# Single-precision mixing of probabilities and values in the second attention of a gated cross-attention kernel

## What is computed

```python
xn = layer_norm(x, g_x, b_x)                  # x: the context, [32, 77, 128]
ln = layer_norm(latents, g_l, b_l)            # latents: the normalised rows, [32, 128, 128]
q = jnp.einsum('bnd,de->bne', ln, Wq)
kv = jnp.einsum('bnd,de->bne', jnp.concatenate([xn, ln], axis=1), Wkv)
k, v = jnp.split(kv, 2, axis=-1)              # then split into 16 heads of 64
sim = jnp.einsum('bhid,bhjd->bhij', q * scale, k)     # 128 queries, 77 + 128 keys
attn = jax.nn.softmax(sim, axis=-1)
out = jnp.einsum('bhij,bhjd->bhid', attn, v)          # the mixing
out = out.transpose(0, 2, 1, 3).reshape(b, m, INNER) @ Wout
return layer_norm(out, g_o, b_o)
```

## Time and profile before

| | us |
|---|---|
| three executions | 1363.77, 1361.43, 1364.35 (median 1363.77) |
| profiled execution | 1359.99 |
| its span (first to last instruction) | 1358.2 |
| PE busy | 1036.5 (76%) |
| POOL busy | 889.6 (65%) |
| DVE busy | 874.3 (64%) |
| ACT busy | 859.2 (63%) |
| `attention1`: first `scores_by_key` to the last one | 478.4 to 1083.6 |
| routing tail up to the first expert tile | 1083.6 to about 1162 |
| experts | about 1162 to the end |

### The profile page before, as it was taken

How to read it: one execution, slowest core, us unless ns; L and a number is a source line. 1 busy time by engine, 2 the same in 40 slices (tenths; PEclk the granted TensorE clock), 3 DMA queues, 4 the chain that set the end, 5 groups by cost and what they waited for, 6 DMA issues and landing times. The chain is left out here.

```text
span 1358.2 us, 36485 instructions
## 1 busy us (share of the span) xinstructions
PE 1036.5 (76%) x13317; PEld 814.9 (60%) x13317; DVE 874.3 (64%) x2471; ACT 859.2 (63%) x1791; POOL 889.6 (65%) x1065
## 2 busy tenths in 40 slices
PE   1568999967894499999999999899999920566660
PEld 1445777753552278887777778777777820355550
DVE  5788788876877766666666656566665611344445
ACT  0568899964663478888877778787777810233330
POOL 1160899964767456677788888888888976144441
PEclk9869555558996599999999999999999965888985
DMA  9993000000221001112112121211212111322215
GB/s 219 261 283 85 10 16 17 16 16 12 44 43 28 1 17 34 32 28 43 33 37 50 31 59 33 53 33 38 52 34 53 33 48 48 56 58 60 63 45 187
DMA packets 210051, 78.40 MB, mean 58 GB/s; under 512 B 149663, under 2 KB 206154, under 8 KB 209883
## 3 DMA queue, kind: packets, MB, share of 16 engines
q1 hardware_dynamic: 179467, 61.91, 21.1%
q10 hardware_dynamic: 25872, 5.56, 2.3%
q0 software_dynamic: 4544, 8.67, 2.0%
HBM read 14.15 MB, written 30.47 MB: 33 GB/s over the span
## 5 line engine op out<-in xcount | busy, mean ns | idle before, releaser
L1671 DVE TENSOR_REDUCE attention_negmax<-bank 128x2 f16<-128x410 f32 x256 | 137.7, 579 | 166.3 <-PE bank L1423 164.4
L1223 POOL TENSOR_TENSOR attention_pl_l<-attention_probs_l,attention_ph_l 128x512 f16<-128x512 f32 x128 | 148.3, 1159 | 97.3 <-ACT attention_ph_l L1552 95.6
L636 POOL TENSOR_TENSOR attention_probs_l<-attention_probs,attention_probs_h 77x512 f16<-77x512 f32 x128 | 145.3, 1152 | 52.8 <-ACT attention_probs_h L718 48.5
L1223 POOL TENSOR_TENSOR attention_pl_c<-attention_probs_c,attention_ph_c 77x512 f16<-77x512 f32 x128 | 147.8, 1154 | 0.0
L1984 POOL DMA_INDIRECT outputs<-experts_y_rows,experts_ids x78 | 77.5, 994 | 102.4 <-ACT experts_y_rows L1921 87.3
L1406 PE MATMUL bank<-layer_kv,ah 128*128 128x128 f16 x1024 | 108.7, 220 | 11.7 <-PEq L2062 11.5
L1438 PEld LDWEIGHTS bank<-identh,attention_negmax 128*128 128x128 f16 (+1 forms) x1024 | 83.3, 107 | 55.9 <-issue 0.3
L1452 PE MATMUL bank<-attention_vh_l,attention_ph_l 128*128 128x65 f16 x512 | 96.0, 195 | 18.2 <-POOL attention_pl_c L1223 18.2
L1406 PE MATMUL bank<-v1h,layer_kv 128*128 128x256 f16 (+1 forms) x512 | 106.4, 275 | 1.3 <-DVE attention_vl_c L1678 1.3
L1665 DVE SCALAR_TENSOR_TENSOR attention_tl<-bank,attention_th 128x512 f16<-128x512 f32 x128 | 87.8, 686 | 28.8 <-ACT attention_th L1543 28.7
L1552 ACT ACTIVATE attention_probs_l<-bank 128x512 f32<-128x512 f32 x128 | 76.2, 595 | 38.3 <-PE bank L1438 36.4
(11 more groups left out here) (367 smaller groups left out, 4150.1 us busy)
## 6 DMA issues: line engine op xcount, KB each, us to landing
tokens<-blank SPq DMA_DIRECT2D x1, 18360.0 KB, 71.0
experts_both<-outputs SPq DMA_DIRECT2D x8, 512.0 KB, 5.2
X<-in_x SPq DMA_DIRECT2D x4, 512.0 KB, 9.4
attention_pay<-attention_pay SPq DMA_DIRECT2D x8, 256.0 KB, 2.8
out<-X ACTq DMA_DIRECT2D x8, 256.0 KB, 4.3
attention_turned_h<-attention_heads_h SPq DMA_TRANSPOSE x96, 2.2
attention_turned_l<-attention_heads_l SPq DMA_TRANSPOSE x96, 2.4
outputs<-experts_y_rows,experts_ids POOLq DMA_INDIRECT x78
```

What stands on the lines that cost most here:

```text
L636: pool.tensor_tensor(probs_l[:, n % SLOTS], probs[:, n % 2], probs_h[:, n % SLOTS], ALU.subtract).then_inc(p_split, 1)
L1223: last = pool.tensor_tensor(low[:, g % 2], whole[:, g % 2], high[:, g % 2], ALU.subtract)
L1671: last = dve.tensor_reduce(negmax[:, g, 2 * i:2 * i + 2], score[i], AX.X, ALU.max, negate=True)
```

## The change

The exponentials are written once, in single precision, by ACT. The values are written once, in single precision, by ACT. The fp16 tiles of both are gone; with them POOL's `probs_low`, DVE's `values_low`, and the semaphores `p_split` and `v_hi`. `v_out` is now raised by ACT. `mix_values` waits for `exped_l` and `exped_c` in place of `p_split`, and makes two products of single-precision operands for each head in place of six fp16 products. Nothing is moved in the order of the steps.

```diff
-        ph_l, ph_c = m.sb("ph_l", [S, 2, HG, S], FP16), m.sb("ph_c", [C, 2, HG, S], FP16)
-        pl_l, pl_c = m.sb("pl_l", [S, 2, HG, S], FP16), m.sb("pl_c", [C, 2, HG, S], FP16)
-        vh_l, vh_c = m.sb("vh_l", [S, 2, H, DK1 + 1], FP16), m.sb("vh_c", [C, 2, H, DK1 + 1], FP16)
-        vl_l, vl_c = m.sb("vl_l", [S, 2, H, DK1 + 1], FP16), m.sb("vl_c", [C, 2, H, DK1 + 1], FP16)
+        vals_l, vals_c = m.sb("vals_l", [S, 2, H, DK1 + 1]), m.sb("vals_c", [C, 2, H, DK1 + 1])
...
                 for g in range(G):
-                    if b < B:
-                        probs_low(b, g)
                     if g == 1 and 1 <= b <= B:
...
             def mix_values(b, g, u):
-                pe.wait_ge(p_split, b * G + (g + 1))
+                pe.wait_ge(exped_l, b * G + (g + 1))
+                pe.wait_ge(exped_c, b * G + (g + 1))
                 pe.wait_ge(v_out, b * G + (g + 1))
...
                 for h in range(HG):
                     v = HG * g + h
-                    products = [(ph_l[:, g % 2, h], vh_l[:, u, v]), (ph_l[:, g % 2, h], vl_l[:, u, v]), (pl_l[:, g % 2, h], vh_l[:, u, v]),
-                                (ph_c[:, g % 2, h], vh_c[:, u, v]), (ph_c[:, g % 2, h], vl_c[:, u, v]), (pl_c[:, g % 2, h], vh_c[:, u, v])]
-                    for i, (x, y) in enumerate(products):
-                        last = pe.matmul(mix[:, h], x, y, start=i == 0, stop=i == len(products) - 1)
+                    pe.matmul(mix[:, h], probs_l[:, g % 2, h], vals_l[:, u, v], start=True, stop=False)
+                    last = pe.matmul(mix[:, h], probs_c[:, g % 2, h], vals_c[:, u, v], start=False, stop=True)
...
-                if late(b * G + g, 2):
-                    act.wait_ge(p_split, b * G + (g - 1))
-                for dst in (probs_l, ph_l):
-                    last = act.activation(dst[:, g % 2], by_key_l, ACT.Exp)
-                last.then_inc(exped_l, 1)
+                act.activation(probs_l[:, g % 2], by_key_l, ACT.Exp).then_inc(exped_l, 1)
                 act.wait_ge(shifted, 2 * (b * G) + (2 * g + 2))
-                for dst in (probs_c, ph_c):
-                    last = act.activation(dst[:, g % 2], by_key_c, ACT.Exp, bias=w.mask_bias[:, 0, b:b + 1])
-                last.then_inc(exped_c, 1)
+                act.activation(probs_c[:, g % 2], by_key_c, ACT.Exp, bias=w.mask_bias[:, 0, b:b + 1]).then_inc(exped_c, 1)
...
-                for dst, src in ((vh_l, v_l), (vh_c, v_c)):
+                for dst, src in ((vals_l, v_l), (vals_c, v_c)):
...
-                last.then_inc(v_hi, 1)
+                last.then_inc(v_out, 1)
...
-                    if n + VALUES_AHEAD < UNITS:
-                        values_low(*unit(n + VALUES_AHEAD))
```

More of the change, by code:

```diff
@@ L1172, in attention1 @@
         turned_x = [m.sem(f"turned_x{u}") for u in range(2)]
-        (ones_in, t_done, t_hi, t_lo, scored, maxed, shifted, exped_l, exped_c, p_split, v_done, v_hi, v_out, mixed, normed, heads_hi,
+        (ones_in, t_done, t_hi, t_lo, scored, maxed, shifted, exped_l, exped_c, v_done, v_out, mixed, normed, heads_hi,
          heads_lo, projected, out_copied, out_read, out_normed, scaled, summed, x_read, biased, nchain, chain) = (
             m.sem(n) for n in ("ones_in", "t_done", "t_hi", "t_lo", "scored", "maxed", "shifted", "exped_l", "exped_c",
-                               "p_split", "v_done", "v_hi", "v_out", "mixed", "normed", "heads_hi", "heads_lo", "projected",
+                               "v_done", "v_out", "mixed", "normed", "heads_hi", "heads_lo", "projected",
                                "out_copied", "out_read", "out_normed", "scaled", "summed", "x_read", "biased", "nchain", "chain"))
@@ L1217, in _ @@
         def _(pool):
-            def probs_low(b, g):
-                if late(b * G + g, 2):
[L1220 to L1224, removed]
             def add_bias(k):
@@ L1531, in _ @@
             scores(0, 0, 0)
-            pe.wait_ge(ones_in, 4)
+            pe.wait_ge(ones_in, 2)
             for g in range(2, VALUES_AHEAD):
@@ L1672, in maximum @@
                 last.then_inc(maxed, 1)
[L1674 to L1680, removed]
             def normalise(b, g, u):
@@ L1789, in body @@
                         places(k)
-            for x, value in ((vh_l, 1.0), (vh_c, 1.0), (vl_l, 0.0), (vl_c, 0.0)):
-                dve.memset(x[:, :, :, DK1:DK1 + 1], value).then_inc(ones_in, 1)
+            for x in (vals_l, vals_c):
+                dve.memset(x[:, :, :, DK1:DK1 + 1], 1.0).then_inc(ones_in, 1)
             for g in range(2):
                 t_low(0, g, 0)
-                values_low(0, g, 0)
             maximum(0, 0, 0)
-            for g in range(2, VALUES_AHEAD):
-                values_low(0, g, 0)
             sequences(body)
```

## The result

The changed kernel takes 1454.89 us (median of four, 1454.02 to 1456.11) against 1362.6 for the kernel before on the same chip: slower by a ratio of 1.068 (95% interval 1.066 to 1.070), or 92.3 us. The forecast was 1465, the range 1442 to 1500. The profiled execution took 1454.02 with a span of 1452.3, which is 94.1 more than the span of the earlier trace rows.

A forecast was written before the change was run, and what follows sets the result against it. PE was taken to bound the second attention: +129.8 us of mixing, less waits of 12.5, 9.5 and 2.2 and a tail of 2.3, made +103.3 on 1359.99, or 1463. Allowing for the median gave 1465, range 1442 to 1500.

The forecast's parts named there:

- PE bounds the stage: Second attention: PE busy 574.6 of 604 us sets the pace; relieving other engines is worth only what PE waits for them.
- Two records a product: Mixing: each single-precision product is two PE records of about 0.112 us, priced by weight load; fewer moving columns don't help.
- The mixing at 1.76 us: Each unit's mixing on PE: 16 records take 1.76 us in place of 0.73, +129.8 us over 126 units.
- The waits: -24.2 in the stage: PE's waits saved in the second attention: 12.5 us for POOL, 9.5 before the projection, 2.2 for a transposing DMA.
- the wait before the projection: PE's 13.0 us for DVE's copy of the gates, six times about 2.1: forecast -9.5, between 0 and -13.
- The cause of the waits' going: Second attention: PE's waits shrink because the work causing them leaves POOL, DVE and ACT or comes earlier.
- The tail: -2.3: Behind the last unit: POOL's two subtractions leave its queue, -2.3 us, between 0 and -5; PE's other 3.4 no gain.
- The new waits for the exponentials: `mix_values` waiting for `exped_l` and `exped_c`: costed at nothing, at most 0.6 us a unit.
- rival 1: Mixing priced by columns moved, at most 0.057 us a record: 1361 us, or 1308 at the fp16 pace; chance 0.04.
- rival 2: Mixing: load and movement in turn, 0.165 us a record, 2.64 a unit: about 1575 us; chance 0.03.
- rival 3: Second attention: the clock falls; a tenth of the stage at the lower clock gives 1495 to 1525 us; chance 0.07.
- Rival 4: PE's waits stay because something else ends them: +27 us at most, 1492; chance 0.07.

The follow-up runs named there:

- e1: The changed kernel with 33 moving value columns in place of 65 in each product of the mixing: 1451.16 us.
- e2: The changed kernel with 200 moving columns in place of 65 in each product of the mixing: 1582.22 us.
- e5: The kernel before with only the mixing's products made single precision, all other work kept and the low-part tiles single-buffered: 1476.59 us.
- e4: The changed kernel with fp16 tiles for probabilities and values, low parts left out: 1318.62 us, 0.967 of the kernel before.
- e3: The changed kernel with 64 stationary columns in place of 128 in each product of the mixing: 1385.86 us.
- e6: e4 with PE's scores of the next unit put ahead of `make_t`: 1271.72 us.

## Why the prediction was right, point by point

- **PE bounds the stage, the rest doesn't.** Right. PE went from 95% to nearly 100% busy in it, while the other three were idle for longer. Their busy time fell by less than I had written (ACT 113 us, not 163; DVE 81, not 106; POOL 287, not 296): mine were sums of durations, which did fall by 167, 104 and 297 us in the two traces, and back-to-back instructions overlap.
- **Two records a product, 0.112 us each, set by the weight load.** Right to the nanosecond for the distance, and the three sizes show the cause. The weak part of the argument was line 282, whose 128 moving columns cost about as much as its load; line 254 with its two columns carried the decision, and e1 confirms what it said. It rested on a lower clock that I inferred: the profile's clock row reads 1.00 there, but its first record of the clock is at 48.4 us, and the transposes of line 274 start 0.213 us apart just before that moment and 0.109 behind it, which bears the inference out. That a record moves its columns at half the fp16 pace was taken from transposes whose own load could have been the price; only e2 shows it for a product.
- **The mixing at 1.76 us, +1.03 a unit.** Measured 1.755 and +1.018 over all quiet units: 128.3 us in place of 129.8. The make-up was a little different: I had the first record full, the last one short (0.06), and 0.02 for the first load; the trace has the first short (0.080) and the last as long as the others (0.112). That these errors cancel is luck.
- **The waits: -24.2 in the stage.** This is the term that was mis-sized. The stage grew by 96.2 where the units' growth is 128.3, so about 32 us went. Of the 8 us in excess, 2 are the wait before the projection: I had left 3.5 us of it (my own terms, about 1 less 0.66, make 2) and 1.6 stayed. The wait view of before lists 29.5 us in all and that of after 2.9, so it shows 26.6 of the 32. About 1 us more is a short stretch at the lower clock in the execution before, behind a stretch in which PE was busy for half of the time:

```profile
775.00:778.50 3.50, 1.76 (x23) 1.32 (x21) 2.35 (x7) 2.61 (x5) 3.10 (x3) 1.00 0.57 44
779.00:782.20 3.20, 3.20 (x32) 2.45 (x31) 1.20 (x3) 0.56 (x3) 3.00 (x4) 0.50 0.28 63
```

  The two units that hold it lose 3.8 us against the changed kernel, where four other pairs of the same kind lose 2.7 to 3.1. The rest may be in how the wait view counts: it takes PE as idle only from the modelled end of the last matmul, which lies up to 0.2 us behind the point from which the next could have started, and nineteen waits of before would make nearly 4 us of that. This last part is reckoned and not shown.
- **The cause of the waits' going.** Half right: with the work put back (e5), 18.5 of the 32 us came back in the stage, some 3 of them in the units with the lower clock. The rest went by the slower PE, which my sum did not name. The wait for the gates needed both (e4, e5).
- **The tail: -2.3, only POOL's subtractions and not the 5.7 us that PE waited.** Near in size (-3.1), but no run tests the mechanism. The stretch from the last unit's start to the end lasts 271.6 to 273.8 us in the seven kernels without low parts and 274.7 to 276.4 in the four with them, so the single difference of two traces is good to about 2 us.
- **The new waits for the exponentials cost nothing.** Right; no wait before lines 1437 and 1438 but one, for DVE's normalisation (0.8 us, behind the last unit).
- **The sum: +103.3 against the profiled execution, +94.0 measured** (1454.02 - 1359.99). The 9 us between are the 8 of the waits, 1.5 of the units and 0.8 of the tail, less 0.9 at the stage's beginning. The further 3.8 us for the median were half added; the kernel before came out at 1362.6 in the larger sample, so a third of that was not there either. The lower end of my range is a slip: records at 0.100 us (-23) and 10 us of waits would reach to about 1432, not 1442. It did not matter here.
- **Rivals.** The price by columns (rival 1, with the four passes of the Trainium skill's page "FP8 and Floating Point Precision", section "TensorE Precision Notes") is refuted at 65 columns by the changed kernel itself, and e1 shows why. Its count of the movement, two passes for each of the two records, fits at 200 columns, where by the estimate above a record would need 0.169 us and 0.168 to 0.172 is read; at 65 it would give 0.055 where 0.112 is read. Load and movement in turn (rival 2) would be 0.165 at 65 columns, where 0.112 is read, and near 0.27 in e2. The clock (rival 3) stayed full in the stage. Rival 4 was refuted: the waits went. A rival that I had not named, a price fixed for each single-precision record, is refuted by e3.

## What to carry to other kernels

A product of single-precision operands cost PE two records here, each with a slow load of its stationary operand (191 ns against 97). With 128 stationary columns a record took 0.112 us at 33, 65 and 128 moving columns, and 0.170 at 200. At 65 columns the load is the price, and three fp16 products from high and low parts (3 x 0.0304 = 0.091 us) are cheaper than one single-precision product (0.223). Before work is taken from an engine, look at who waits for it: here 480 us of busy time on ACT, POOL and DVE were removed and PE got back some 32 us of waits, part of them only because it had become slower itself. And where PE gets faster in such a ring of steps, ask at once which short step of another engine its work had covered (e4, e6).

## What the runs showed of the hardware that I had not expected

- At 200 moving columns load and movement overlap fully: 0.168 to 0.172 us a record, where the movement alone is 0.169 by the estimate above, and 0.112 at 33 and 65 columns is the load.
- A mixing with 64 stationary columns between fp16 steps of 128 paid about 0.1 us on either side (0.152 us from its last record to the next start, and 0.45 us for the four matmuls ahead of it in place of 0.36).
- The fp16 record behind single-precision ones starts 0.112 us after the last of them, though it needs only a short load and the last one moves 65 columns.
